# An attention block on one core: residual rows in a ring of six tiles, two pairs of the next batch projected early, and new orders of the steps

## The reference

```python
scale_shift = emb @ W_emb + b_emb
scale, shift = jnp.split(scale_shift, 2, axis=-1)
xn = _rms_norm(x, g_norm) * (1.0 + scale) + shift
qkv = xn @ W_qkv                      # 1024 x 3072, 16 heads of 64
q = _rms_norm(q, g_q); k = _rms_norm(k, g_k)
logits = jnp.einsum('bhqd,bhkd->bhqk', q, k) * d ** (-0.5)
attn = jax.nn.softmax(logits, axis=-1)
o = jnp.einsum('bhqk,bhkd->bhqd', attn, v)
return x + (o + o @ W_out)
```

## Time and profile before

| | us |
|---|---|
| median of three runs | 2371.29 (2369.93 to 2376.03) |
| the profiled execution, its own time | 2372.36 |
| its span, from first to last instruction | 2370.6 |
| PE (TensorE matmuls) busy | 2293.4, 97% |
| PE weight loads busy | 2122.5, 90% |
| VectorE busy | 1601.7, 68% |
| ScalarE busy | 1343.9, 57% |
| GpSimd busy | 655.6, 28% |
| DMA, share of the 16 engines | 40% |
| granted clock of PE, mean | 0.991 |

### The profile page before, as it was taken

The page is one execution under the profiler, slowest core; times in us unless marked ns, Lnnn a source line. Parts: engine busy times, 40 slices in busy tenths (PEclk is TensorE's granted clock), DMA queues, the critical chain, the costliest instruction groups (busy, mean ns, idle before and its releaser), DMA issues.

```text
span 2370.6 us, 41536 instructions
## 1 busy us (share of the span) xinstructions
PE 2293.4 (97%) x13392; PEld 2122.5 (90%) x13392; DVE 1601.7 (68%) x3267; ACT 1343.9 (57%) x3101; POOL 655.6 (28%) x884
## 2 busy tenths in 40 slices
PE   7999999999999999999999999999999999999988
PEld 3998998999998999999999999989999899999977
DVE  2698787477845778367873678737787277863772
ACT  3677775366734676256761667625675266743660
POOL 2553432223203232033320333212321224212210
PEclk8999999999999999999999999999999999999999
DMA  7744225623255232553236332364323632335223
GB/s 284 258 178 170 107 96 182 233 107 131 81 187 220 100 116 86 182 196 108 107 111 215 138 107 107 121 237 149 118 76 128 254 112 107 107 126 198 107 104 97
DMA packets 85638, 346.70 MB, mean 146 GB/s; under 512 B 7600, under 2 KB 59824, under 8 KB 63920
## 3 DMA queue, kind: packets, MB, share of 16 engines
q1 hardware_dynamic: 85424, 344.01, 40.0%
HBM read 293.65 MB, written 50.33 MB: 145 GB/s over the span
## 4 chain that ended last, share of the span: by engine, by line
PE 78%; DVE 7%; DMA 6%; issue 5%; ACT 3%; POOL 1%; SPq 1%; ACTq 0%; DVEq 0%; POOLq 0%
PE proj_bank L469 16%; PE proj_bank L471 16%; PE proj_bank L470 16%; PE flip_bank L526 8%; PE pv_bank L535 4%; PE pv_bank L536 4%; PE score_bank L518 4%; PE score_bank L519 4%; DVE neg_max L751 2%; PE flip_bank L491 2%; DMA res<-in_x 2%; DMA x_tile<-in_x 2%; DMA out<-res 1%; DVE probs L757 1%; DMA w_raw<-in_w_out 1%
## 5 line engine op out<-in xcount | busy, mean ns | idle before, releaser
L469 PE MATMUL proj_bank<-w_split,xn_hi 128*128 128x384 f32 x2048 | 701.9, 343 | 12.5 <-DVE qk_stage L778 6.5
L471 PE MATMUL proj_bank<-w_split,xn_lo 128*128 128x384 f32 x2048 | 690.2, 337 | 0.0
L470 PE MATMUL proj_bank<-w_split,xn_hi 128*128 128x384 f32 x2048 | 689.3, 337 | 0.0
L635 ACT ACTIVATE probs<-score_bank,neg_max 128x512 f32<-128x512 f32 x512 | 352.0, 692 | 242.3 <-DVE neg_max L751 231.5
L761 DVE TENSOR_TENSOR pt_lo<-flip_bank,pt_hi 128x512 fp32r<-128x512 f32 x512 | 340.0, 687 | 123.0 <-ACT pt_hi L641 119.7
L469 PEld LDWEIGHTS proj_bank<-w_split,xn_hi 128*128 128x128 f32 x2048 | 386.4, 189 | 36.0 <-DVE qk_stage L778 9.8
L470 PEld LDWEIGHTS proj_bank<-w_split,xn_hi 128*128 128x128 f32 x2048 | 386.7, 189 | 17.5
L641 ACT CAST pt_hi<-flip_bank 128x512 fp32r<-128x512 f32 x512 | 286.8, 591 | 177.7 <-PE pv_bank L536 109.3
L471 PEld LDWEIGHTS proj_bank<-w_split,xn_lo 128*128 128x128 f32 x2048 | 385.9, 188 | 0.0
L751 DVE TENSOR_REDUCE neg_max<-score_bank 128x1 f32<-128x512 f32 x512 | 337.6, 684 | 35.3 <-PE score_bank L519 32.8
L526 PE MATMUL flip_bank<-ident,probs 128*128 128x128 f32 x2048 | 285.3, 274 | 15.1 <-DVE pt_lo L761 9.9
(11 more groups left out here) (70 smaller groups left out, 3172.1 us busy)
## 6 DMA issues: line engine op xcount, KB each, us to landing
w_split<-w_store SPq DMA_DIRECT2D x140, 1536.0 KB, 6.9
w_store<-w_split SPq DMA_DIRECT2D x20, 1536.0 KB, 10.0
x_tile<-in_x SPq DMA_DIRECT2D x32, 512.0 KB, 11.4
w_split<-w_store SPq DMA_DIRECT2D x14, 1024.0 KB, 6.0
w_raw<-in_w_qkv SPq DMA_DIRECT2D x16, 768.0 KB, 7.6
res<-in_x SPq DMA_DIRECT2D x64, 192.0 KB, 2.6
out<-res SPq DMA_DIRECT2D x64, 192.0 KB, 2.4
emb_stage<-in_w_emb SPq DMA_DIRECT2D x5, 1024.0 KB, 11.0
```

What stands on the lines that cost most here:

```text
L469: nc.tensor.matmul(dst, a_hi, w_hi, start=(kt == 0), stop=False)
L470: nc.tensor.matmul(dst, a_hi, w_lo, start=False, stop=False)
L471: mm = nc.tensor.matmul(dst, a_lo, w_hi, start=False, stop=(kt == KT - 1))
L635: nc.scalar.activation(probs[h][:, i, :], score_bank[n % 2][:, :], ACT.Exp, bias=neg_max[:, n:n + 1], accum_out=row_sum[:, n:n + 1]).then_ ...
```

## The change

- `LATE` is 2: only pairs 8 and 9 are projected before the output product, and the next list begins with all of pair 2.
- Residual rows: in the first batch three tiles as before (`first_res`); from the second on a ring of six tiles in `w_raw`. Nine pairs of semaphores instead of three.
- Split weights lie without gaps: a slot of n columns fills `KT * 2 * n` elements of the buffer and of `w_store`. Only the 256-column slot lies otherwise than before. Its second half lies elsewhere too, so the first weight load behind it (slot LATE + 1) waits for the whole output product and not for its first half.
- In the head, `cond_sb` is loaded behind the first tile of W_emb and has a semaphore of its own; the four other constants are loaded behind the x tiles.
- All lists of steps are new. In TAIL, P4, P5 and P6 go ahead of P3.

```diff
-LATE = 3
+LATE = 2
 BODY, TensorE (before, then after: the start, and from 9C12)
-        3C0 3C1 3C2 3C3 2W0 2W1 3C4 3C5 2F4 2F5 2W2 2W3 3C6 3C7 3C8 2F6 2F7 2W4 2W5 3C9 3C10 2W6 2W7 3C11 3C12 3C13 3C14
-        3C15 4C0 4C1 4C2 4C3 3T0 3T1 4C4 4C5 4C6 4C7 4C8 4C9 3S0 3S1 4C10 4C11 3S2 3S3 4C12 4C13 3S4 3S5 4C14 3F0 3F1
...
-        10C7 9S2 10C8 9S3 10C9 10C10 9S4 10C11 9S5 9F0 9F1 10C12 9S6 10C13 9F2 9F3 9S7 9W0 9W1 10C14 10C15 9W2 9W3 9F4
-        9F5 P0 P1 9F6 10T0 9W4 9W5 P2 P3 10T1 9W6 P4 9F7 P5 P6 P7 10S0 9W7 10S1 P8 P9 10S2 10S3 P10 P11 10S4 10S5 10F0
-        10F1 P12 P13 10F2 10F3 10S6 10S7 P14 P15 P16 P17 P18 P19 P20 P21 P22 P23 P24 P25 P26 P27 P28 P29 P30 P31 P32 P33
+        2C0 2C1 2C2 2C3 2C4 2C5 2C6 2C7 2C8 2C9 2C10 2C11 2C12 2C13 2C14 2C15 3C0 3C1 3C2 3C3 2T0 2T1 3C4 3C5 3C6 3C7
+        3C8 3C9 2S0 2S1 3C10 3C11 2S2 2S3 3C12 3C13 3C14 2S4 2S5 3C15 2F0 2F1 4C0 2S6 2S7 4C1 2F2 2F3 2W0 2W1 4C2 4C3
...
+        8F1 8S6 9C13 8S7 9C14 8F2 8F3 8W0 8W1 9C15 P0 8F4 8F5 8W2 8W3 P1 P2 9T0 9T1 8W4 8W5 P3 P4 8F6 P5 P6 P7 8F7 8W6
+        9S0 9S1 P8 8W7 P9 9S2 9S3 P10 P11 9S4 9S5 P12 9F0 9F1 P13 9S6 9S7 P14 9F2 9F3 9W0 9W1 P15 P16 9F4 9W2 9F5 9W3
+        P17 9F6 9W4 9F7 9W5 P18 9W6 P19 9W7 P20 P21 P22 P23 P24 P25 P26 P27 P28 P29 P30 P31 P32 P33 P34 P35 P36 P37 P38
 BODY, ScalarE, the start
-        +A0 2F4 2F5 2O0 +A1 3D1 +A2 2F6 2F7 +A3 2O1 3D2 2Q0 3D3 3V0 3V1 4D0 3T0 3T1 4D1 3S0 3S1 4D2 3S2 3S3 3S4 3F0 3F1
+        0Q0 1Q0 2D0 2D1 2D2 2D3 2V0 2V1 3D0 2T0 2T1 3D1 +A0 2S0 2S1 +A1 3D2 +A2 2S2 2S3 +A3 2S4 2S5 2F0 2F1 3D3 2S6 2S7
 BODY, SyncE
-        4W1 +X0 +X1 +X2 +X3 -O11 E1 E2 5W0 5W1 6W0 6W1 7W0 7W1 8W0 8W1 9W0 9W1 10W0 10W1 W0 W1 W2 W3 O0 E3 O1 E4 O2 W4
-        E5 W5 O3 E6 O4 E7 O5 E8 O6 11W0 11W1 E9 O7 O8 E10 O9 E11 12W0 +E0 O10""".split(),
+        E2 E3 E4 3W1 E5 4W0 4W1 +X0 +X1 +X2 +X3 5W0 5W1 6W0 6W1 7W0 7W1 8W0 8W1 9W0 9W1 W0 W1 W2 W3 O0 E6 O1 E7 O2 W4 E8
+        W5 O3 E9 O4 E10 O5 E11 O6 10W0 +E0 10W1 O7 O8 O9 O10 11W0 +E1 O11""".split(),
 HEAD, SyncE, the end
-        7G0 6H0 7G1 6H1 E0 E1 E2 G0 7H0 G1 7H1 8W0 8W1 9W0 9W1 10W0 10W1 G2 H0 G3 H1 G4 H2 O0 G5 H3 E3 O1 E4 O2 E5 O3 H4
-        H5 E6 O4 E7 O5 E8 O6 11W0 11W1 E9 O7 O8 E10 O9 E11 12W0 +E0 O10""".split(),
+        7G0 6H0 7G1 6H1 E0 E1 E2 G0 7H0 G1 7H1 8W0 8W1 9W0 9W1 G2 H0 G3 H1 G4 H2 G5 H3 O0 O1 E3 E4 O2 E5 O3 H4 E6 H5 O4
+        E7 O5 E8 O6 10W0 E9 10W1 O7 O8 O9 E10 E11 +E0 +E1 11W0 O10 O11""".split(),
 HEAD, VectorE, around I0
-        4F2 4F3 7L3 5M3 6D0 4S7 +B0 4O0 6M0 5T0 4N7 5T1 I0
+        7L3 4F6 5T0 6D0 5T1 4F7 6M0 5S0 6D1 5S1 4O1 5N0 5N1 I0
 TAIL, TensorE, the end
-        5F0 5F1 5S6 6C14 5F2 5S7 5F3 5W0 5W1 6C15 7C0 5W2 5W3 7C1 5F4 5F5 7C2 7C3 6T0 6T1 5W4 5W5 7C4 7C5 5F6 7C6 7C7
-        7C8 5F7 5W6 6S0 6S1 7C9 5W7 7C10 6S2 6S3 7C11 7C12 6S4 6S5 7C13 6F0 6F1 6S6 7C14 6F2 6S7 6F3 6W0 6W1 7C15 P0 6W2
-        6W3 P1 6F4 6F5 P2 7T0 6W4 7T1 6W5 6F6 6F7 7S0 6W6 7S1 6W7 7S2 7S3 7S4 7S5 7F0 7F1 7S6 7F2 7S7 7F3 7W0 7W1 7W2
-        7W3 7F4 7F5 7F6 7W4 7F7 7W5 7W6 7W7 P3 P4 P5 P6 P7 P8 P9 P10 P11 P12 P13 P14 P15 P16 P17 P18 P19 P20 P21 P22 P23
+        7C8 5F5 5F6 5W4 6S0 6S1 5F7 5W5 5W6 7C9 7C10 5W7 6S2 6S3 7C11 7C12 6S4 6S5 7C13 6F0 6F1 7C14 6S6 6S7 7C15 6F2
+        6F3 6W0 6W1 P0 P1 6F4 6W2 7T0 6W3 P2 7T1 6W4 P4 6F5 P5 P6 6F6 7S0 6F7 6W5 7S1 6W6 7S2 7S3 6W7 7S4 7S5 7F0 7F1
+        7S6 7S7 7F2 7W0 7F3 7W1 7W2 7F4 7F5 7W3 7F6 7W4 7F7 7W5 7W6 7W7 P3 P7 P8 P9 P10 P11 P12 P13 P14 P15 P16 P17 P18

-    w_store = nc.dram_tensor("w_store", (SLOTS, P, KT, 2, QKV), F32, kind="Internal").ap()
+    w_store = nc.dram_tensor("w_store", (SLOTS, P, KT * 2 * QKV), F32, kind="Internal").ap()
-        w_split = [sb(f"w_split{i}", [P, KT, 2, QKV], F32R) for i in range(2)]
+        w_split = [sb(f"w_split{i}", [P, KT * 2 * QKV], F32R) for i in range(2)]
+        def split_view(w, n):
+            return w_split[w][:, 0:KT * 2 * n].rearrange("p (k c n) -> p k c n", c=2, n=n)
+        def res_tile(b, g):
+            if is_first(b):
+                return first_res[g % 3][:, :], g % 3, g // 3
+            return w_raw[:, g % NRES, :], 3 + g % NRES, b * (NOUT * TT // NRES) + (g // NRES - NOUT * TT // NRES)
 load_split
-                if half == 0:
+                if half == 0 and slot != LATE + 1:
                     sp.wait_ge(w_used, count(kept) * (KT - 1) + 4)
                 else:
                     sp.wait_ge(proj_done, count(kept) * TT + TT)
 load_res (store_out likewise)
-                sp.wait_ge(res_stored[g % NRES], (m * 2 + c) * (16 * NOUT * TT // NRES) + 16 * (g // NRES + 1))
+                res, at, uses = res_tile(m * 2 + c, g)
+                sp.wait_ge(res_stored[at], uses * 16 + 16)
 head
-                (cond_sb[:, :, :], cond_t),
-            for dst, src in nc_const:
-                sp.dma_start(dst, src).then_inc(const_loaded, 16)
             emb_rows = w_emb.rearrange("(k p) (c n) -> k p c n", p=P, n=512)
             for kt in range(KT):
...
                 sp.dma_start(emb_tile[slot], emb_rows[kt]).then_inc(emb_loaded[slot], 16)
+                if kt == 0:
+                    sp.dma_start(cond_sb[:, :, :], cond_t).then_inc(cond_loaded, 16)
...
             for r in range(TT):
                 load_x(0, 0, r)
+            for dst, src in nc_const:
+                sp.dma_start(dst, src).then_inc(const_loaded, 16)
```

More of the change, by code:

```diff
@@ new lines @@
+        6F3 6W1 6F4 6W2 8C12 7S2 6F5 7S3 6W3 6F6 6W4 8C13 6F7 6W5 8C14 6W6 7S4 7S5 6W7 7F0 7F1 8C15 7S6 7S7 9C0 7F2 7F3
+        7W0 7W1 9C1 9C2 7W2 9C3 8T0 8T1 7W3 9C4 9C5 9C6 9C7 7F4 9C8 9C9 7F5 7F6 7W4 8S0 8S1 7F7 7W5 9C10 7W6 8S2 9C11
+        7W7 9C12 8S3 8S4 9C13 9C14 8S5 8S6 8F0 8F1 9C15 P0 8F2 8F3 8W0 8W1 8S7 P1 P2 9T0 9T1 8W2 8W3 P3 P4 P5 P6 8F4 P7
+        P8 8F5 8F6 8W4 9S0 9S1 8F7 8W5 P9 8W6 P10 8W7 9S2 9S3 P11 P12 9S4 9S5 P13 9F0 9F1 P14 9S6 9S7 P15 9F2 9F3 9W0
+        9W1 P16 P17 P18 9F4 9F5 9W2 9W3 P19 P20 9F6 9F7 9W4 9W5 P21 P22 9W6 9W7 P23 P24 P25 P26 P27 P28 P29 P30 P31 P32
@@ new lines @@
+        7W2 7W3 9C3 9C4 7F4 9C5 9C6 9C7 7F5 7F6 7W4 8S0 8S1 7F7 7W5 7W6 9C8 9C9 7W7 8S2 8S3 9C10 9C11 8S4 8S5 9C12 8F0
+        8F1 8S6 9C13 8S7 9C14 8F2 8F3 8W0 8W1 9C15 P0 8F4 8F5 8W2 8W3 P1 P2 9T0 9T1 8W4 8W5 P3 P4 8F6 P5 P6 P7 8F7 8W6
+        9S0 9S1 P8 8W7 P9 9S2 9S3 P10 P11 9S4 9S5 P12 9F0 9F1 P13 9S6 9S7 P14 9F2 9F3 9W0 9W1 P15 P16 9F4 9W2 9F5 9W3
+        P17 9F6 9W4 9F7 9W5 P18 9W6 P19 9W7 P20 P21 P22 P23 P24 P25 P26 P27 P28 P29 P30 P31 P32 P33 P34 P35 P36 P37 P38
+        P39 P40 P41 P42 P43 P44 P45 P46 P47""".split(),
@@ new lines @@
+        6C12 6C13 5S4 6C14 5S5 5F0 5F1 6C15 5S6 5S7 7C0 5F2 5F3 5W0 5W1 7C1 7C2 7C3 6T0 6T1 5W2 5W3 7C4 7C5 5F4 7C6 7C7
+        7C8 5F5 5F6 5W4 6S0 6S1 5F7 5W5 5W6 7C9 7C10 5W7 6S2 6S3 7C11 7C12 6S4 6S5 7C13 6F0 6F1 7C14 6S6 6S7 7C15 6F2
+        6F3 6W0 6W1 P0 P1 6F4 6W2 7T0 6W3 P2 7T1 6W4 P4 6F5 P5 P6 6F6 7S0 6F7 6W5 7S1 6W6 7S2 7S3 6W7 7S4 7S5 7F0 7F1
+        7S6 7S7 7F2 7W0 7F3 7W1 7W2 7F4 7F5 7W3 7F6 7W4 7F7 7W5 7W6 7W7 P3 P7 P8 P9 P10 P11 P12 P13 P14 P15 P16 P17 P18
+        P19 P20 P21 P22 P23 P24 P25 P26 P27 P28 P29 P30 P31 P32 P33 P34 P35 P36 P37 P38 P39 P40 P41 P42 P43 P44 P45 P46
@@ L179 @@
-        E11 O10 O11""".split(),
+        E2 E3 E4 3W1 E5 4W0 4W1 5W0 5W1 6W0 6W1 7W0 7W1 W0 W1 W2 W3 O0 O1 E6 E7 O2 W4 E8 W5 O3 O4 E9 E10 O5 E11 O6 O7 O8
+        O9 O10 O11""".split(),
 }
@@ L335, in cond_attention @@
         o_pair = sb("o_pair", [P, T])
-        NRES = 3
-        res = [sb(f"res{i}", [P, 384]) for i in range(NRES)]
+        first_res = [sb(f"res{i}", [P, QKV]) for i in range(3)]
         ident = sb("ident", [P, P])
@@ L974, in _ @@
             ]
[L975 to L978 removed]
+            for stored in res_stored:
+                sp.sem_inc(stored, 16)
             emb_rows = w_emb.rearrange("(k p) (c n) -> k p c n", p=P, n=512)
```

249 lines of the change are left out of this document (121 added, 128 removed).

## The result

The changed kernel takes **2308.16 us** (median of four runs, 2307.03 to 2310.12), the kernel before 2373.09 us on the same chip: a ratio of 0.9727, 95% interval 0.9711 to 0.9744. Forecast were 2338 us and a range of 2327 to 2358. The direction was right; the gain was 62.3 us of span (2370.6 to 2308.3) where the sum had 33.2.

What follows compares the result with a forecast made beforehand. PE, busy 97% of the span, was taken as the bound, leaving 77 us idle and its clock falls to gain. The terms summed to -33.2 us from 2370.6: span 2337.4, median 2338 us, range 2327 to 2358.

Steps and rivals of the forecast that it cites:

- R: Batch boundaries: PE's waits for the drain's addition (`res`), late for residual rows, go with the ring of six: -17.4 us.
- F, issue and M: Start of next batch: PE's waits for `pt_lo`, issue and `qk_stage` go with two pairs early instead of three: -10.0 us.
- x tile: Next batch's x tile lands late, delaying ScalarE's square and an exponential by 1.0 us at six boundaries: +6.0 us.
- clock: Three falls of PE's clock behind boundary stalls go, 1.8 us each: -5.4 us; one more in the head: -1.8 us.
- denser attention: Attention at 16.0 pieces a pair instead of 17.1 adds steady-part gaps, 1.0 us a batch: +7.0 us.
- constants: Kernel start: W_emb loads ahead of the five constants, so PE starts earlier: -2.1 us.
- head: First batch: waits for `pt_lo` (-2.1), its clock fall (-1.8) and `k_lo` (-1.7) go; new gaps add +1.5 us.
- tail: Last batch: six output pieces instead of three fill PE's idle time in the last pair: -3.1 us.
- Rival 1: Freed time returns as small attention gaps, one more in each of some 48 pairs: 2355 us; chance 0.13.
- Rival 2: The x tile becomes the new wait, the present 5.2 us paid by PE in six batches: 2357 us; chance 0.10.
- Rival 3: Attention is bound by its own latency, so pairs take 1 us more: slower, 2394 us; chance 0.06.
- Rival 4: The change misses the wait: residual rows stay late, stalls only move, about 2368 us; chance 0.09.

Runs made afterwards that it cites:

- b_mid: Kernel before with the changed kernel's order of the middle steps on all engines, `LATE`, boundary and loads kept: 2359.63 us, ratio 0.9934.
- b_swap: Kernel before with one projection piece put between transposes and scores at two places of TensorE's list, 4F1/4S6 and 5F1/5S6: 2369.72 us, ratio 0.9981.
- a_xfirst: Changed kernel with the next batch's x tiles loaded ahead of weights 4W0 and 4W1 in the middle batches: 2306.63 us, ratio 0.9714.
- a_tail: Changed kernel with P4, P5 and P6 back behind P3 in the last batch: 2312.00 us, ratio 0.9734.
- b_: Prefix of all edits made to the kernel before; their medians run from 2348.50 to 2369.72 us.
- a_const: Changed kernel with the five constants loaded ahead of the first W_emb load again: 2310.45 us, ratio 0.9728.

## Why the prediction was right or wrong

By its own terms, each against the columns of the first table:

| term of the sum | forecast | measured |
|---|---|---|
| boundary, from 9C15 on: R -17.4, F, issue and M -10.0, x tile +6.0, clock -5.4 | -26.8 | -30.6 |
| middle, to 9C15: denser attention | +7.0 | -12.1 |
| group changes on PE (work) | -4.1 | -4.6 |
| constants (start to X0) | -2.1 | -3.4 |
| head: `pt_lo` -2.1, clock -1.8, `k_lo` -1.7, new gaps +1.5 | -4.1 | -8.8 |
| tail | -3.1 | -3.0 |
| sum | -33.2 | -62.5 |

(Cut at 8F0, as the first table's columns are, it would be -26.6 and -16.1.)

**The step that failed is "Denser attention".** It said that a pair at 16 pieces looks like the steady part of before, gaps of 0.38 us included, and added one such gap per batch. One new gap a batch did come, of 0.62 us behind 8F1. The failure is that the old gaps were put down as staying. b_mid shows that a new order of the same steps, at the same number of pieces, removes them: they stood behind fixed steps, 2.8 us a batch (7T1 0.83, 4F1 and 5F1 0.62 each, 6S6 0.38, 5F7 0.27). Old and new together it is -12.5 us in b_mid where I had +7.0. That a gap belongs to its two neighbouring steps was tested alone for two of them (b_swap): one went whole, and half of the other moved to the next step. I had the rows before me, 18 gaps for `probs` and six for `qk_stage` at the same step each time, and costed their staying instead of looking which neighbours the new lists put there. 19 of the 29 us of error are this step. Most of the head's missing 4.7 us are of the same kind: in the first batch of before 3F1 to 3S6 and 4F1 to 4S6 lose 0.6 and 0.5 us, 7T1 to 8C8 0.85, P11 to 10S0 1.8, and none of these is there after. That part is read from the trace, and no run isolates it.

**Gaps weigh more than they show.** Before 4S6 the trace has 0.38 us idle; the step comes 0.65 us behind the last transpose, start to start, where 0.03 is the time without a wait, so 0.62 are lost. The Trainium skill (Perfetto Trace Analysis, Summary: the profiler window per engine type) says that the profile gives TensorE's instructions from their prefetch start to an estimated end. The trace fits that: the busy sum of PE fell by 21.1 us with the same matmuls, of which the shorter time at 1.2 GHz explains 7 at most. A sum over waits, as mine, understates what is to be had. Start-to-start times of steps don't.

**The boundary came out within 4 us, with its parts off: partly luck.** The ring was worth 13.1 us in spans and not 17.4, since the next wait took up the rest; the new lists took more than the 10.0 forecast (13.7, or 17.7 from 9C15 on). +6.0 us for the x tile were wrong: in the fourth batch 4W0 was issued 14.8 us behind T (14.6 forecast), ScalarE asked for X0 at T+26.7 (26.4) and had it at T+27.9 (29.0), so it was late as I had worked it out, by 1.3 us:

```profile
1261.86 1.06 ACT L586 ACTIVATE square_out<-x_tile 128x1024 bf16<-128x1024 f32 x1 [1.30 <-DMA x_tile<-in_x]
```

But it ends inside the pieces beside it, and a_xfirst shows that PE pays nothing. Against that the loop's 4.0 us stayed, which I had taken for something else: the 1.7 us of `issue` were to go with F and W of pair 2, and the 1.38 us at the other return were among the 17.4 of the ring. Both are the return of the loop, in the kernel before as after, and only writing it out removes them. The forecast of no clock fall in the body failed with them in the profiled execution. X0 landed 13.1 us after 4W0's issue: the trace's 14.4 was the better guide than the 10.0 that I had worked out from the fit of the Trainium skill (DMA: Bandwidth & Descriptors, Anatomy of one DMA), an estimate which, with 1536 KB twice and 512 KB, should have read 10.4.

**Constants, tail, split weights** were right in place, and in size by their columns. In the tail that is partly luck: a_tail prices the three pieces at 4.5 us, so the rest of the new list there took 1.5 back. Six executions with the constants first (b_ and a_const) have X0 at 41.1 to 41.7 us, six others with the changed start at 38.7 to 40.8, so -3.4 is -1.4 in the mean of six against six, and the rest the luck of two executions.

**The rivals.** Rival 1 (freed time comes back as small gaps) had one such gap a batch, and more of them went than came. Rival 2 had its wait, at a quarter of its size, and no cost. Rival 3 needed a pair to take over 28.9 us whatever stands beside it; the period of a batch fell by 7 us. Rival 4 fell with the residual waits. Of the signs, `res`, `pt_lo` and VectorE's wait came as said; ScalarE's wait for the x tile was smaller (5.1 us in all, where 2 to 3 a batch were forecast). That there would be no clock fall between 250 and 2290 us did not come true, with two behind the loop and two among the last pair's steps (2245.6 and 2262.6).
